# A graph layer's edge loop: a fifth group of rows picked by TensorE, edge rows in four places, and a ring of rows that shrinks in two steps

## The reference, cut to what matters

```python
h = relu(layernorm(x))
edge_feat = mlp(edge_attr, W_edge, ...)               # 4 -> 96, relu, batch norm over all edges
message = concat([h[src], h[dst], edge_feat], axis=1) # (E, 288)
message = mlp(message, W_msg, ...)                    # relu(m @ W + b), batch norm over all edges
agg = segment_sum(message, dst, N)
out = x + agg + mlp(h, W_node, ...)
```

## Time and profile before

| | |
|---|---|
| time before, median of 3 runs | 996.21 us (996.05 to 1000.87) |
| the profiled execution's own time | 996.7 us |
| its span, from the first to the last instruction | 994.9 us |
| PE / DVE / ACT / POOL busy | 774.8 / 662.0 / 381.6 / 716.9 us |
| mean granted TensorE clock | 0.911 of full |

### The profile page before, as it was taken

One profiled execution on the slowest core, in us unless ns is written; L12 is line 12 of the kernel. 1 busy time (PEld: TensorE's weight loads), 2 busy tenths in 40 slices (PEclk: granted clock), 3 DMA queues, 4 the chain that ended last, 5 costly groups with the idle time before them and its releaser, 6 DMA issues.

```text
span 994.9 us, 21739 instructions
## 1 busy us (share of the span) xinstructions
PE 774.8 (78%) x4750; PEld 624.3 (63%) x4822; DVE 662.0 (67%) x1590; ACT 381.6 (38%) x648; POOL 716.9 (72%) x762
## 2 busy tenths in 40 slices
PE   1734687567258898888788789899989999987898
PEld 1604562222148787787777778777777777776684
DVE  8577878778735555555577756767766766665555
ACT  2843696667323333333444433222222222222230
POOL 6777777777777777774777777777777777777750
PEclk9957795766569999999999999999999999999999
DMA  9575533333633333333444333232323233222223
GB/s 296 132 283 156 127 73 80 77 74 80 166 68 74 73 72 76 74 74 67 92 101 102 80 85 70 63 76 64 66 65 76 64 67 76 65 63 64 57 56 98
DMA packets 102661, 91.30 MB, mean 92 GB/s; under 512 B 73638, under 2 KB 78390, under 8 KB 102409
## 3 DMA queue, kind: packets, MB, share of 16 engines
q1 hardware_dynamic: 76144, 51.04, 19.2%
q0 software_dynamic: 24256, 37.31, 17.4%
q10 hardware_dynamic: 2136, 1.62, 0.6%
HBM read 72.00 MB, written 14.54 MB: 87 GB/s over the span
## 4 chain that ended last, share of the span: by engine, by line
SPq 29%; PE 20%; issue 16%; POOL 11%; DMA 9%; DVE 8%; ACT 4%; ACTq 3%; DVEq 0%; POOLq 0%
SPq L581 14%; POOL ring L625 11%; PE pd L972 6%; SPq L529 4%; DMA xs<-x_stack 4%; PE pc L961 4%; PE pb L984 3%; DMA ring<-p_table,src_idx 3%; SPq L574 3%; PE pc L859 3%; SPq L515 2%; DVE ring L1313 2%; ACTq L806 2%; DMA big_a<-zeros 2%; SPq L404 2%
## 5 line engine op out<-in xcount | busy, mean ns | idle before, releaser
L625 POOL DMA_INDIRECT ring<-p_table,src_idx x710 | 670.9, 945 | 226.7 <-issue 196.4
L972 PE MATMUL pd<-hm 128*97 128x193 f32 x1564 | 295.2, 331 | 0.9 <-ACT hm L792 0.9
L972 PEld LDWEIGHTS pd<-hm 128*97 128x97 f32 x1564 | 247.9, 167 | 5.1 <-ACT hm L792 1.2
L961 PE MATMUL pc<-w3q,r_sb 128*128 128x96 f32 x1564 | 208.3, 277 | 46.3 <-DMA xs<-x_stack 16.4
L961 PEld LDWEIGHTS pc<-w3q,r_sb 128*128 128x128 f32 x1564 | 204.0, 194 | 52.2 <-ACT r_sb L782 26.1
L782 ACT ACTIVATE r_sb<-pa 128x512 f32<-128x512 f32 x196 | 116.7, 596 | 305.6 <-issue 163.8
L1268 DVE TENSOR_TENSOR gram<-gram,pd 97x97 f32<-97x97 f32 x196 | 50.2, 256 | 163.7 <-PE pd L972 149.8
L792 ACT ACTIVATE hm<-pc 128x384 f32<-128x384 f32 x196 | 96.2, 491 | 156.9 <-DVE pc L1262 149.3
L1262 DVE TENSOR_TENSOR pc<-pc,ring 128x384 f32<-128x384 f32 x194 | 108.6, 560 | 61.2 <-PE pc L961 32.0
L1165 DVE BATCH_NORM_STATS2 edge_st<-r_sb 96x512 f32 (+1 forms) x196 | 121.3, 675 | 36.1 <-ACT r_sb L744 34.7
L984 PE MATMUL pb<-ring 128*128 128x288 bf16 x784 | 114.2, 290 | 24.5 <-DVE ring L1313 24.4
(11 more groups left out here) (125 smaller groups left out, 494.7 us busy)
## 6 DMA issues: line engine op xcount, KB each, us to landing
w3q<-q_table SPq DMA_DIRECT2D x782, 11.2 KB
ring<-p_table,src_idx POOLq DMA_INDIRECT x710
ln_buf<-p_table ACTq DMA_DIRECT2D x704, 0.4 KB
xs<-x_stack SPq DMA_DIRECT2D x98, 72.0 KB
x_stack<-ring SPq DMA_DIRECT2D x6, 980.0 KB, 5.6
xs<-x_stack SPq DMA_DIRECT2D x98, 60.0 KB
ln_buf<-p_table SPq DMA_DIRECT2D x320, 0.4 KB
ring<-in_x_nodes SPq DMA_DIRECT2D x5, 480.0 KB, 9.1
```

Source lines behind the costliest of these rows:

```text
L625: nc.gpsimd.indirect_dma_start(out=ring[:, tile * C:(tile + 1) * C], out_offset=None, in_=table, in_offset=bass.IndirectOffsetOnAxis(ap=id ...
L961: last = nc.tensor.matmul(pc[:, j % 2, t * C:(t + 1) * C], r_sb[:, j % 2, t * TILE:(t + 1) * TILE], w3q[:, j, t, :], start=True, stop=True)
L972: last = nc.tensor.matmul(pd[0:M1, j % 2, 0:HW], hm[:, j, t, WIN:HW], hm[:, j, t, :], start=(t == 0), stop=(t == n - 1))
```

## The change

NEAR gets a fifth group (185 to 189), so TensorE picks 20 tiles and POOL fetches one group less. A tile takes four groups of the loop and not five, with turns (3, 2, 2, 0) and not (2, 2, 2, 1, 0); both end at group 185. The edge rows get four places, filled two pairs of groups ahead; SP's wait for a place at its step g asks for the same count as before, `edge_lin` >= g - 2. The ring goes from 60 slots to MID = 37 for groups 97 to 125 and to 29 only after, since the stage becomes three small buffers (15 blocks) in the place where the whole table stood, and the near things move to the front of the late region. The stage loads of SP come one group later and wait for the buffer three back (`low_made`); SP's source numbers and DVE's hots get waits for the slots below 37 to be free.

```diff
-LATE = 29
+MID, LATE = 37, 29
+STAGES = 3
-NEAR = tuple(range(FAR[0] - 4, FAR[0]))
+NEAR = tuple(range(FAR[0] - 5, FAR[0]))
-NEAR_AT, NEAR_GAP = 106, 5
-HOT_TURNS = (2, 2, 2, 1, 0)
+NEAR_AT, NEAR_GAP = 106, 4
+HOT_TURNS = (3, 2, 2, 0)
...
-        x_main = [sem(f"x_main{k}") for k in range(2)]
+        x_main = [sem(f"x_main{k}") for k in range(4)]
...
-            return g if g < RING else (g - RING) % LATE
+            return g if g < RING else g - RING if g < RING + MID else (g - RING - MID) % LATE
+
+        def slot_freed(g):
+
+            return g + 1 - (RING if g < RING + MID else MID if g < RING + MID + LATE else LATE)
...
+                def load_edges(pair):
+
+                    if pair < NG // 2:
+                        wait(sp, edge_lin, 2 * pair - 6)
+                        sp.dma_start(xs[0:KX, pair % 4, :], x_stack[:, bass.ts(pair, 2 * GROUP)]).then_inc(
+                            x_main[pair % 4], 16)
+
+                load_edges(0)
+                load_edges(1)
                 for g in range(NG):
                     i, j = at(0, g)
                     if g % 2 == 0:
-
-                        wait(sp, edge_lin, g - 2)
-                        sp.dma_start(xs[0:KX, j // 2, :], x_stack[:, g * GROUP:(g + 2) * GROUP]).then_inc(
-                            x_main[j // 2], 16)
+                        load_edges(g // 2 + 2)
...
-                    for c in part_step(g, -3):
+                    for c in part_step(g, -2):
                         sp.wait_ge(pre_added, RING)
+                        wait(sp, low_made, c + 1 - STAGES)
                         rows = p_table[c * PART_B * P:min((c + 1) * PART_B, NN) * P, :]
-                        sp.dma_start(stage[:, part_blocks(c), :], rows.rearrange("(b p) c -> p b c", p=P)).then_inc(
+                        sp.dma_start(stage(c), rows.rearrange("(b p) c -> p b c", p=P)).then_inc(
                             stage_in[c], 16)
...
                             sp.wait_ge(low_made, PARTS)
+                            sp.wait_ge(pre_added, RING + MID)
                             wait(sp, near_hot, (k - 1) * TPG * HOTS)
...
-                        wait(pool, pre_added, g + 1 - (RING if g < RING + LATE else LATE))
+                        wait(pool, pre_added, slot_freed(g))
...
                         dve.wait_ge(near_placed, tile // TPG + 1)
+                        dve.wait_ge(low_made, PARTS)
+                        dve.wait_ge(pre_added, RING + MID)
                         wait(dve, near_used, n + 1 - HOT_BUFS)
```

More of the change, by code:

```diff
@@ L122, in graph_layer @@
         late = ring[:, LATE * TPG * C:RING * TPG * C]
[L123 to L128, removed]
+        parts_at, stage_at = late.shape[1] - NN * 3 * C // 2, (MID - LATE) * TPG * C
+        parts = late[:, parts_at:].bitcast(bf16).rearrange("p (b s c) -> p b s c", s=3, c=C)
+        stages = late[:, stage_at:stage_at + STAGES * PART_B * C].rearrange("p (k b c) -> p k b c", k=STAGES, c=C)
+        near_at = HOT_BUFS * HOT_B * P // 2
+        hots = late[:, 0:near_at].bitcast(bf16).rearrange("p (k b e) -> p k b e", k=HOT_BUFS, b=HOT_B)
+        near_f = late[:, near_at:near_at + 2 * GROUP].rearrange("p (k e) -> p k e", k=2)
         near_src = late[:, near_at:near_at + 2 * GROUP].bitcast(i32).rearrange("p (k e) -> p k e", k=2)
-        near_f = late[:, near_at:near_at + 2 * GROUP].rearrange("p (k e) -> p k e", k=2)
         near_at += 2 * GROUP
         near = late[:, near_at:near_at + NEAR_T * C]
+        assert near_at + NEAR_T * C <= parts_at and stage_at + STAGES * PART_B * C <= parts_at
         big_a = sb("big_a", [P, NP])
@@ L362, in part_blocks, with stage @@
             return slice(c * PART_B, min((c + 1) * PART_B, NN))
+        def stage(c):
+            return stages[:, c % STAGES, 0:min(PART_B, NN - c * PART_B), :]
         def part_scratch(c):
@@ L817, in _ @@
                         act.wait_ge(stage_in[c], 16)
-                        nc.scalar.copy(parts[:, part_blocks(c), 0, :], stage[:, part_blocks(c), :]).then_inc(high_made, 1)
+                        nc.scalar.copy(parts[:, part_blocks(c), 0, :], stage(c)).then_inc(high_made, 1)
                     for c in part_step(g, 2):
                         act.wait_ge(high_off, c + 1)
-                        nc.scalar.copy(parts[:, part_blocks(c), 1, :], stage[:, part_blocks(c), :]).then_inc(mid_made, 1)
+                        nc.scalar.copy(parts[:, part_blocks(c), 1, :], stage(c)).then_inc(mid_made, 1)
                     for tile in near_tile(g + 2, 0):
@@ L944, in edges @@
                     if j % 2 == 0:
-                        pe.wait_ge(x_main[j // 2], i * 16 + 16)
+                        pe.wait_ge(x_main[g // 2 % 4], g // 8 * 16 + 16)
                     wait(pe, edge_relu, g - 1)
                     nc.tensor.matmul(pa[:, j % 2, 0:n * TILE], we_stack[:, :],
-                                     xs[:, j // 2, j % 2 * GROUP:j % 2 * GROUP + n * TILE],
+                                     xs[:, g // 2 % 4, j % 2 * GROUP:j % 2 * GROUP + n * TILE],
                                      start=True, stop=True).then_inc(edge_lin, 1)
@@ L1289, in near_parts @@
                         dve.wait_ge(part_copied, 2 * c + 1)
-                        V.tensor_tensor(stage[:, part_blocks(c), :], stage[:, part_blocks(c), :], part_scratch(c),
+                        V.tensor_tensor(stage(c), stage(c), part_scratch(c),
                                         ALU.subtract).then_inc(high_off, 1)
@@ L1295, in near_parts @@
                         dve.wait_ge(part_copied, 2 * c + 2)
-                        V.tensor_tensor(parts[:, part_blocks(c), 2, :], stage[:, part_blocks(c), :], part_scratch(c),
+                        V.tensor_tensor(parts[:, part_blocks(c), 2, :], stage(c), part_scratch(c),
                                         ALU.subtract).then_inc(low_made, 1)
```

## The result

| | before | after |
|---|---|---|
| time, median of 4 runs | 997.49 us (996.05 to 1000.87) | 1014.54 us (1010.76 to 1017.79) |
| span of the profiled execution | 994.9 us | 1012.9 us |
| its own time | 996.7 us | 1015.42 us |
| PE / DVE / POOL busy | 774.8 / 662.0 / 716.9 us | 803.2 / 692.1 / 713.6 us |

A forecast was written before the change was run, and what follows sets the result against it. SP's issuing bounds the kernel up to group 105, then PE and DVE, last POOL. The terms 603.3, 361.0, 4.8, 26.0, 17.8 and 1.8, less 0.5 for the median, gave 1014.2 us; range 1001 to 1025.

The forecast's parts named there:

- the time of groups 106 to 185: PE and DVE pace these groups: 20 tiles of 18.05 us, 361.0 us in all.
- POOL's saving goes nowhere: POOL's gathers end 15 us earlier, but group 184's rows only lie in the ring; no gain in time.
- The price of a third turn: In steps with three turns, one turn more adds 1.0 us to 4.85, giving 5.85 us.
- up to group 105: SP's issuing paces this stretch, staying at 5.97 us a pair; gram row of group 105 at 603.3 us.
- the bounds of 598 to 607: Forecast limits, in us, for the start of group 105's gram row.
- the two waits: Two more DVE waits before each hot cost 0.08 us in 60 steps: 4.8 us (0 to 20).
- the tail: The last ten gram rows, after group 185, take 26.0 us (24.0 to 28.1).
- The two late relus: After group 185, two sets of far loads stand before ACT's relus: 2 x 3.6 us against 4.8.
- first stage: The edge loop up to group 105, paced by SP; forecast to end at 603.3 us.
- output: From the last gram row to the span's end: 17.8 us, as before.
- POOL paces the end: Rival: consumer reaches group 184 when POOL does, as PE's edge-row waits were latency; 983.4 us, faster; chance 0.11.
- More per step: Rival: waits before the first hot cost 0.2 us or more, or relus are late; 1026 us; chance 0.09.

The follow-up runs named there:

- e4: The changed kernel with DVE building the next group's near hots before it adds the window sums, not after: 984.42 us, ratio 0.9851.
- e1: The changed kernel with four near groups again, 16 tiles in five groups each with the old turns: 989.21 us, ratio 0.9905.
- e8: The changed kernel with MID = 29, so the ring shrinks in one step at group 89 as before: 1014.42 us, ratio 1.0144.
- e9: The kernel before with only the ring in two steps; sixteen tiles and two edge-row places stay: 986.28 us, ratio 0.9872.
- the second: The kernel before, unchanged, run once more for another profile: 999.54 us, group 105 at 605.35 us.
- e11: The changed kernel with four edge-row places but each load one pair of groups ahead, not two: 1013.22 us, ratio 1.0130.
- e3: The changed kernel with the two new waits before each hot given three times, four waits more: 1024.47 us, ratio 1.0246.
- e2: The kernel before with only the edge rows changed, to four places loaded two pairs ahead: 1000.38 us, ratio 1.0012.
- e5: The changed kernel with SP reading 16 registers once in four groups, not 8 once in two: 1003.61 us, ratio 1.0044.
- e6: The changed kernel with the edits of e4 and e5 together: 985.05 us, ratio 0.9857.
- e12: The changed kernel with edge rows in two places as before and DVE's hots before its window sums: 984.85 us, ratio 0.9861.

## Why the prediction was right, and where its terms were off

**Right: the time of groups 106 to 185.** Steps of 5.85, 4.85, 4.85 and 2.39 were forecast, and 361.0 us for 20 tiles; measured are 5.86, 4.85, 4.85, 2.39 and 361.2. The price of a third turn, 1.0, came from one PE row and one DVE row that overlap. Of the two it is DVE's: PE's 1.02 a turn was no price of its own, since e4 has it at 0.86 where the hots are ready. e1 shows the other side: with the old turns the same ring and edges are 26.4 us shorter, all of it here.

**Right: POOL's saving goes nowhere.** The wait is gone, the last gather ended at 946.8 (947 forecast), and the rows of group 184 were there at 929.3, while its add came at 961. e8 takes the saving away at no cost. The ring that doesn't fill is worth something where POOL is the late side (e9: 13 us against before, with the old turns), but the fifth near group is paid by the engines that were next in line. What one fetched group less is worth by itself, no run shows alone.

**Wrong term: up to group 105.** I said that SP's 5.97 us a pair stay, and put group 105 at 603.3; it came at 609.1. The step at fault is "Per pair it issues the same DMAs and waits for the same count", with its "So its 5.97 us a pair stay." The start came 0.9 us later (0.8 forecast), and PE came 1.4 us closer behind SP against the first profile of before, as forecast (only 0.4 against the second). But SP took 321.9 us for its 53 pairs where it had taken 316.2. SP's waits in this stretch (us, times, longest), and the line of its edge loads after:

```profile
SPq L580 <- PE pa L964: 3.1, 3, 1.6
SPq L596 <- PE pc L978: 0.4, 1, 0.4
```
```profile
L580 SPq DMA_DIRECT2D xs<-x_stack x56: 325/376/1850, 279.2 to 602.1; - x56
```

Three waits of up to 1.6 us are new (0.3 in all before), and one load took 1.85 us to issue where the longest had been 1.06. Over the profiles with the registers read as before, SP's 53 pairs took 316.2 to 320.0 us with two places (five profiles, mean 318.1) and 320.4 to 322.7 with four (seven, mean 321.8). So four places cost SP 3.7 us between the means, and my 5.97 a pair was the lowest of five samples: about 1.9 of the 5.7 us are scatter of one execution against another. Which of its parts makes SP slower is open. No one kind of instruction has it: between the profiles of before and after, all `w3q` loads together grew by 2.0 us (149.1 to 151.1) and the edge loads by 1.7 (21.1 to 22.8). One profile of e11, at 322.4 us, speaks against the distance and against the new waits, which are 0.5 us there. One profile is a poor source for a pace that goes over 300 us; the bounds of 598 to 607 that I drew from it were too narrow.

**Wrong term: the two waits.** Forecast 4.8 us (0 to 20), measured 0. The Trainium skill, page "VectorE: DVE Perf Modes", section "The DRAIN you can't avoid", gave 0 for them, and this trace agrees for the two of the change. e3 doesn't: four more cost 0.17 us each time, so "nothing extra" isn't a price for any number of waits. That the first two hide behind the agg add, which runs in that gap, fits the rows but wasn't tested by itself.

**Nearly right: the tail.** 26.0 us forecast, 25.2 measured. The two late relus cost less: the steps of groups 186 and 187 are 3.11 and 2.83 us, 1.1 over two plain ones of 2.4, since the first of them came earlier than I took: ACT's relu started at 970.28, with the gram row of 185, where before it had started 1.7 us after that row (950.63). The errors against the forecast of 1014.7 for the profiled execution are +5.8 (first stage), +0.2 (tiles), -4.8 (waits), -0.8 (tail), -0.4 (output, 17.4 us) and +0.7 (2.5 us around the span where there had been 1.8): 0.7 in all. They nearly cancel, and that is luck: the two largest, the first stage and the waits, have nothing to do with each other. The total is much closer than its parts.

**The rivals.** POOL paces the end: refuted for the change (no wait for POOL), and e2 refutes the source it needed: PE's 35.6 us of waits for edge rows went, and came back before the products. The Trainium skill, page "SBUF — State Buffer", section "The DMA setup-cost knee", has each transfer pay about 2 us; no run here shows that figure, and e2 and e5 show why it doesn't decide: loads that are issued late by a full queue come late however early they stand in it, and the stage moves only when the queue has less to issue. More per step: refuted at two waits, and e3 shows what it looks like.

**What was there to be had.** The stall is in the order of DVE's step: PE wants a hot before it is there 47 times in the 80 groups, mostly by 0.43 us, 20.9 us in all. DVE could build it before the window sums, which no engine wants before PE's next window sum. e4 shows it: 36 us less over the 80 groups, more than the 20.9 of these waits. The timelines show where the rest is: in a step with two turns PE takes 0.94 us from the start of its products to the first turn (711.60 - 710.66), where it took 1.46 (711.91 - 710.45), and each further turn takes it 0.86 us and not 1.0. From there POOL is the bound again, and e4, e6 and e12, at 984.4 to 985.1 us, are the fastest versions found. They are within each other's scatter, and e9, without a fifth group, is only some 1 to 2 us behind; e4's order without a fifth group wasn't run, so what the group adds to that order is open.

## What to carry to other kernels

Take work from a producer only where the profile shows the consumer waiting for it, over the whole stretch in which the price is paid: here POOL gave up one group, and the engines that took it were the late side for 60 of the 80 groups. Within a step, put the operation for which another engine waits ahead of the one for which nobody does; that order was worth more than any buffer. A queue that issues without pause wasn't helped here by loading further ahead, only by fewer instructions.

## What the runs showed of the hardware

- Reading registers on SP isn't a fixed cost: 8 take 0.78 us (after) and 16 take 1.24 (e5), so half of the reads save only a fifth of their time.
- With its one-hots ready, PE takes 0.86 us for a turn of 7 matmuls (e4); behind DVE's one-hots, which start 1.0 us apart, a second and a third turn take 1.0.
- Two satisfied waits added between two DVE operations left the start of the second at 0.34 us after the first (before and after); six moved it to 0.51 us (e3).
- One indirect gather of 128 rows every 1.25 us held wherever POOL had no wait, in the profiles of before and after alike.
